# Centring the output projection's weights once, and a residual step without a mean, in an attention and mixture-of-experts block on one Trainium2 core

## The reference, cut to what matters

```python
# x: (8, 512, 256)
x = x + layernorm(attention(layernorm(x)))      # attention ends in: out @ W_o.T
x = x + layernorm(moe_ffn(layernorm(x)))

def layernorm(x, eps=1e-05):
    m = mean(x, -1); v = var(x, -1)
    return (x - m) / sqrt(v + eps)
```

## Time and profile before

| | |
|---|---|
| runs shown | median 965.01 us of 3 (961.19 to 965.33) |
| the profiled execution: its own time | 970.2 us |
| the profiled execution: its span | 968.0 us, mean granted TensorE clock 0.914 |
| busy in the span | PE 811.1 us (84%), DVE 641.1 (66%), ACT 449.8 (46%), POOL 423.0 (44%) |
| DMA | 168.40 MB moved |

### The profile page before, as it was taken

One profiled execution on the slowest core, in us unless ns is written; L12 is line 12 of the kernel. 1 busy time (PEld: TensorE's weight loads), 2 busy tenths in 40 slices (PEclk: granted clock), 3 DMA queues, 4 the chain that ended last, 5 costly groups with the idle time before them and its releaser, 6 DMA issues.

```text
span 968.0 us, 19930 instructions
## 1 busy us (share of the span) xinstructions
PE 811.1 (84%) x6324; PEld 597.3 (62%) x6324; DVE 641.1 (66%) x1850; ACT 449.8 (46%) x731; POOL 423.0 (44%) x408
## 2 busy tenths in 40 slices
PE   3559887887988997897978987989998999888755
PEld 2427464564664764664745555868886888777622
DVE  5686857689688788788687664644643334977616
ACT  2205544645654654654644656545554555444300
POOL 3132213116516427427314335476677655655421
PEclk9758989999998898998997879899999999989878
DMA  4586845335537437436496213554566758888582
GB/s 175 131 206 169 241 92 132 88 88 149 152 99 171 141 98 191 130 85 192 131 334 189 92 49 108 159 182 145 162 213 215 208 163 315 315 289 305 209 348 97
DMA packets 88147, 168.40 MB, mean 174 GB/s; under 512 B 14192, under 2 KB 55664, under 8 KB 87792
## 3 DMA queue, kind: packets, MB, share of 16 engines
q1 hardware_dynamic: 74224, 128.59, 46.0%
q0 software_dynamic: 13824, 38.55, 10.5%
HBM read 90.15 MB, written 76.68 MB: 172 GB/s over the span
## 4 chain that ended last, share of the span: by engine, by line
PE 30%; DVE 9%; DMA 7%; issue 4%; POOL 3%; SPq 3%; ACT 2%; DVEq 0%; POOLq 0%; ACTq 0%
PE ring L1540 9%; PE ring L1561 4%; DMA xg<-sorted_rows 3%; PE ring L1526 2%; DVE nmax L833 2%; POOL expert_rows L736 2%; PE ring L1440 2%; PE ring L1318 2%; PE ring L1320 2%; PE ring L1319 2%; PE ring L1396 2%; DMA q_st<-mrow 2%; DMA expert_rows<-ys,dest 1%; SPq L628 1%; PE ring L1332 1%
## 5 line engine op out<-in xcount | busy, mean ns | idle before, releaser
L736 POOL DMA_INDIRECT expert_rows<-ys,dest x160 | 159.0, 994 | 94.3 <-ACT ys L1199 44.5
L1248 ACT ACTIVATE prob<-ring 128x1024 f32<-128x1024 f32 x128 | 130.1, 1022 | 144.7 <-PE ring L1387 144.3
L833 DVE TENSOR_REDUCE nmax<-ring 128x2 f32<-128x768 f32 (+1 forms) x192 | 158.2, 862 | 26.3 <-PE ring L1369 25.1
L728 POOL DMA_INDIRECT sorted_rows<-xr,idx_all x128 | 126.6, 989 | 96.7 <-DVE xr L995 63.4
L1540 PE MATMUL ring<-we,xh 128*128 x640 | 158.9, 393 | 0.0
L1540 PEld LDWEIGHTS ring<-we,xh 128*128 128x128 f32 x640 | 120.7, 199 | 14.2
L1058 DVE SCALAR_TENSOR_TENSOR sl<-sl,got,ring 128x128 f32<-128x128 f32 x160 | 48.3, 343 | 104.2 <-ACT sl L1300 104.1
L1396 PE MATMUL ring<-prob,v_sb 128*32 128x512 f32 (+3 forms) x1024 | 97.3, 479 | 3.3 <-ACT prob L1248 3.3
L1362 PE MATMUL ring<-k_st,q_st 48*128 48x384 f32 (+3 forms) x512 | 80.4, 374 | 20.9 <-DVE nmax L830 10.3
L706 POOL TENSOR_TENSOR rot<-rot 128x512 f32<-128x512 f32 x14 | 17.9, 1276 | 160.0 <-DVE rot L810 160.0
L1381 PE MATMUL ring<-maskt_b,halves_b 64*128 64x128 bf16 (+2 forms) x640 | 50.7, 238 | 42.2 <-DMA q_st<-mrow 20.7
(11 more groups left out here) (205 smaller groups left out, 1687.7 us busy)
## 6 DMA issues: line engine op xcount, KB each, us to landing
xg<-sorted_rows SPq DMA_DIRECT2D x160, 134.0 KB
parts<-part SPq DMA_DIRECT2D x32, 512.0 KB, 5.8
ykt<-expert_rows SPq DMA_DIRECT2D x14, 1024.0 KB, 10.0
k_st<-parts SPq DMA_DIRECT2D x64, 128.0 KB
q_st<-parts SPq DMA_DIRECT2D x64, 128.0 KB
we<-w_exp SPq DMA_DIRECT2D x1, 6144.0 KB, 21.4
sorted_rows<-zeros SPq DMA_DIRECT2D x2, 2144.0 KB, 9.0
sorted_rows<-zeros SPq DMA_DIRECT2D x32, 134.0 KB
```

The source lines that it names most:

```text
L728: pool.indirect_dma_start(out=xs[group_of(s)], out_offset=bass.IndirectOffsetOnAxis(ap=idx_all[:, s, t, k:k + 1], axis=0), in_=xr[:, s % 2 ...
L736: pool.indirect_dma_start(out=yk, out_offset=bass.IndirectOffsetOnAxis(ap=dest[:, j % 8, b:b + 1], axis=0), in_=ys[:, j % NYS, b, :], in_o ...
L833: dve.tensor_reduce(nmax[:, Q % 2, :, pp, qb], slot[:, :, col:col + (qb + 1) * P], AX.X, ALU.max, negate=True).then_inc(s_max, 1)
L1248: act_e.activation(prob[:, u % 2, 2 * half:2 * half + 2, :], slot[:, :, :], ACT.Exp, scale=SCALE).then_inc(s_exp, 1)
```

## The change

A new function `centre_output_weights` on DVE reduces the `W_o` columns of `stage` (128 partitions, 2 tiles of 256) to their sums, multiplies by 1/256 and subtracts the mean in place. It runs at step "XT" of sequence 0, in the place where `w_lo` was made. ACT's copies to `w_hi` and `w_gate` wait for it and go from step "LNR" to step "QK" of sequence 0. DVE's making of `w_lo` goes from step "XT" to step "V" of sequence 0, which in the plan stands after "LNR" and ahead of "XT" of sequence 1. `residual` becomes four `scalar_tensor_tensor` of 128x256, `x1 = pr * rstd2 + x1`, with both waits ahead of them. The statistics of `pr` stay as they were.

```diff
-N_LN = 5 * NT + 1
+N_LN = 5 * NT
...
             def store_x1(s):
-                sp.wait_ge(s_ln, N_LN * s + 3 * NT + 1)
+                sp.wait_ge(s_ln, N_LN * s + 3 * NT)
...
+            def centre_output_weights():
+                w_o = stage[:, C_O:C_O + KD * D].rearrange("p (k d) -> p k d", k=KD)
+                dve.wait_ge(s_small, 16)
+                dve.tensor_reduce(w_mean[:, 0, :], w_o, AX.X, ALU.add).then_inc(s_centre, 1)
+                dve.wait_ge(s_centre, 1)
+                dve.tensor_scalar(w_mean[:, 1, :], w_mean[:, 0, :], 1.0 / D, None, ALU.mult).then_inc(s_centre, 1)
+                dve.wait_ge(s_centre, 2)
+                dve.tensor_tensor(w_o, w_o, w_mean[:, 1, :].unsqueeze(2).to_broadcast([P, KD, D]),
+                                  ALU.subtract).then_inc(s_centre, 1)
...
             def residual(s):
-                done = N_LN * s + 2 * NT
                 dve.wait_ge(s_lnr, 2 * s + 1)
+                dve.wait_ge(s_x1in, 16 * (s + 1))
                 for t in range(NT):
-                    dve.tensor_scalar(pr[:, t, :], pr[:, t, :], mv2[:, t, 0:1], rstd2[:, t:t + 1],
-                                      ALU.subtract, ALU.mult).then_inc(s_ln, 1)
-                dve.wait_ge(s_x1in, 16 * (s + 1))
-                dve.wait_ge(s_ln, done + NT)
-                dve.tensor_tensor(x1[:, :, :], x1[:, :, :], pr[:, :, :], ALU.add).then_inc(s_ln, 1)
+                    dve.scalar_tensor_tensor(x1[:, t, :], pr[:, t, :], rstd2[:, t:t + 1], x1[:, t, :],
+                                             ALU.mult, ALU.add).then_inc(s_ln, 1)
 
             def residual_statistics(s):
-                done = N_LN * s + 3 * NT + 1
+                done = N_LN * s + 3 * NT
...
                 elif kind == "XT":
                     xt_low(n, ring[RING_SLOT[st]])
+                    if n == 0:
+                        centre_output_weights()
+                elif kind == "V":
                     if n == 0:
                         weights_low(1, slice(C_O, C_GATE), w_hi[:, :], w_lo[:, :])
...
-                elif kind == "LNR" and n == 0:
-                    act_e.wait_ge(s_small, 16)
+                elif kind == "QK" and n == 0 and st[2] == 0:
+                    act_e.wait_ge(s_centre, 3)
                     copy(w_hi[:, :], stage[:, C_O:C_GATE], s_whi)
```

More of the change, by code:

```diff
@@ L328, in block_kernel @@
         r_s = place("r_s", [P, 3, NT])
+        w_mean = place("w_mean", [P, 2, KD])
         cw = place("cw", [P, NT, E])
@@ L400, in block_kernel @@
         s_wlo = sem("weights_low")
+        s_centre = sem("output_weights_centred")
         s_seen_dve = sem("waited_dve")
```

## The result

| | before | changed |
|---|---|---|
| median of 12 runs each | 963.36 us (959.75 to 968.73) | 953.03 us (950.95 to 958.38) |
| ratio, with its 95% interval | | 0.9899 (0.9874 to 0.9923) |
| profiled execution: time, span, clock | 970.2, 968.0, 0.914 | 957.5, 955.3, 0.924 |

The change gains 1.0%. The number came out better than its parts: one term of the sum was too large, the microseconds arrive in other sequences than forecast, and one step of the argument was wrong. Ratios leave out an execution that is over 1.5% above the fastest of its kernel; there is one, in the run with the tiny residual, and it is the one that was profiled.

What follows compares the result with a forecast made beforehand. It took PE and DVE taking turns, with DVE's residual on the path, as the bound. From a median of 965.0 us, -8.4 for seven residuals, +0.4 for the start and -2.6 for the clock gave 954.4, range 948 to 961.

Steps and rivals of the forecast that it cites:

- What bounds the kernel: Steady attention: PE and DVE take turns, the residual lies on the path, with 1.78 us of room on PE's side.
- Sequences 1 to 4 have this same pattern: Periods of sequences 1 to 4: PE waits 1.78 us behind the residual in each, so each saving arrives.
- The residual step: DVE, each residual: 2.62 us before; four multiply-and-adds save 1.26 to 1.06 us, taken as 1.2.
- four new ones move on every 0.34: DVE residual: each new instruction takes a step of 0.34 us, 1.36 us together, from the plain two-tensor operation.
- the far row: Upper bound from a 128x128 multiply-with-pointer with one PSUM operand: 0.39 us per new instruction, four times 1.56.
- The trace does not agree: DVE residual: set aside the skill's rate rule (some 0.5 us less saving per sequence), citing 406 ns against 426.
- How many steps arrive: Eight residuals: the 1.2 us saving arrives in seven, all but sequence 7; 7 x 1.2 = 8.4 us.
- In sequence 7 the saving is nothing: Sequence 7: DVE itself waits 5.28 us for POOL's power, queued behind scatters, so nothing is gained.
- The start: Kernel start: centring and ACT's copy cost 0; moved `w_lo` delays `xt_lo` of sequence 1, +0.4 us, bounds 0 to 2.4.
- The clock: Half-clock stretches behind PE's two waits shrink from 6.6 to 3.4 us in two of five periods: -2.6 us.
- The sum: Whole kernel: -8.4 + 0.4 = -8.0 us, then -2.6 for half-clock stretches; from 965.0 to 954.4 us.
- The slower rival: Every residual meets POOL's two SBUF subtractions on the shared port, 3.3 us instead of 2.62: 970.3 us; chance 0.03.

Runs made afterwards that it cites:

- the tiny residual: The changed kernel with multiply-and-adds on 2 of the 256 channels at each residual; 947.1 us, 0.9817 of the kernel before.
- the filler: The changed kernel with one reduction over 912 elements behind each new residual: 962.32 us, 0.9997 of the kernel before; with two such reductions 975.06 us, 1.0116.
- the start alone: The kernel before with centring and moved weight copies but the old residual; 967.04 us, 1.0042 of the kernel before; run again 966.51 us, 1.0036.
- the two kernels with a later residual: The changed kernel with the residual due at 24.85, not 24.7: 969.09 us, 1.0057 of the kernel before; with statistics and normalised rows later too: 973.63 us, 1.011.

## Why the prediction was right, point by point

- **What bounds the kernel: right.** The residual lay on the path, and the filler shows it from the other side: 1.02 us put back at each residual takes the gain away. The room on PE's side was not the same everywhere, as "Sequences 1 to 4 have this same pattern" has it: in sequence 2 of the profile before, PE ran at half clock from 303.7 to 307.2 and then waited only 0.35 us (at 307.63), not 1.78. The period 2-3 became 1.1 us shorter all the same; the second wait, for line 830, stood there in full (1.97).
- **The residual step: right in kind, one term too large.** "four new ones move on every 0.34" was 0.40 ((1.67 - 0.480) / 3), and the saving 1.02 instead of 1.2, just under my lower bound of 1.06. Seven times that is 7.1 us, not 8.4. I had taken the plain two-tensor operation as nearest and left out that a per-partition scalar has its price; the value from the far row, 0.39, was the better one.
- **"The trace does not agree": wrong.** I set the rule of the Trainium skill (VectorE: DVE Perf Modes, "The perf-mode tier table": `tensor_scalar` at two elements per cycle, `tensor_tensor` at one) aside because the old one took 406 ns and the two-tensor one 426. One size can't tell a rate from a fixed part. The measured growths, 0.40 and 0.80 us for 768 elements, bear the rule out; what the table doesn't give is the 0.13 us for two pointers. By the rule alone the saving would have been some 0.7 us, by my rows 1.2; it was 1.02.
- **How many steps arrive: seven was the wrong picture.** By the table of periods they arrive, with what the clock adds, in sequences 0 to 4 and 6; in sequence 5, for which I had counted a whole one, nothing can be told. Sequence 0 saved 0.9 of its own (4.53 to 3.63). "In sequence 7 the saving is nothing", with DVE's wait longer by the saving, failed: the wait is 5.07 instead of 5.28. POOL's power runs 10.58 us behind the residual's start (625.93) where before it was 11.15 (638.31), because a scatter issue ahead of it in POOL's queue is no longer drawn out by the old addition. With the filler, which is a reduction and no addition, it is 10.58 too. I had priced the port between DVE and POOL in one direction only.
- **The start: harmless, but not by the step I gave.** +0.4 us was forecast, since `w_lo` would end near 39.15 and hold `xt_lo`. DVE came to `w_lo` at 35.87, 0.9 us sooner than I had placed it, for a reason that is not traced, and `xt_lo` ends at 39.45, no later than before. The first residual stands at 161.84 against 161.47, but the kernel before alone gave 161.47 in one profile and 160.13 in another. With the old residual the same start costs 3.5 us, most of it at the addition of sequence 2.
- **The clock: the right kind and size, not the right places.** PE's granted clock is 0.50, 1.2 GHz, behind the two waits before. I had taken shorter stretches for two of five residuals. In the means of three profiles the time at half clock is 3.4 us less in periods 1-2 and 6-7 and 4.6 less in 3-4, but 1.9 more in 4-5 and 5.0 more in 5-6. Single stretches prove little: behind the residual of sequence 5 it is gone in the second profile of the kernel before as well. The whole is a mean of 148 to 153 us for the kernel before in its sets of runs, 135 for the changed one, 151 with one filler, 173 with two, 123 with the tiny residual. Between runs of one kernel a microsecond more at half clock goes with -0.08 to 0.28 us more of span, by which set of 12 or more runs is taken; 13 to 18 us less are worth up to some 5 by that, where I had 2.6. That is an estimate and no proof.
- **The sum.** Mine was 8.4 - 0.4 + 2.6 = 10.6. Seven times the measured 1.02 is 7.1, which leaves 3.2 of the 10.3 us for the clock and sequence 7; that is a subtraction, and how the gain splits stays open. That the total came out within half a microsecond is partly luck: the instruction was overestimated, sequence 5 brought nothing, and sequence 7, the start and the clock brought more than I had.
- **The slower rival: the mechanism is real.** I put the point at who starts first, the residual or POOL's pair. It is met in sequence 0 of every kernel but the tiny one, in sequence 2 of the start alone, and in sequences 0 to 4 of the two kernels with a later residual. The Trainium skill, SBUF — State Buffer, "SBUF: two separate sides", calls this an exclusive lock between the two engines, which whoever starts first keeps for its whole instruction. The runs agree that one engine stands while the other works. Who started first can't be read from the profile's starts alone: the addition at 305.54 started 0.44 us ahead of the pair and still waited for it, and with the later residual a multiply-and-add of 0.48 us started at 234.28, 0.61 ahead of the pair, and ended at 237.70. In both cases POOL was already in the scatter issue that the pair follows without a gap (305.00 and 233.91). Whether that issue holds the port was not tested by itself.

## What to carry to other kernels

To tell what an instruction of another form will cost, take rows of two sizes: one size can't tell a rate from a fixed part, and here it hid both a doubled rate and 0.13 us for two pointers. Before a step on VectorE is shortened, lengthened or moved, look how far GpSimd's next two-tensor operation on SBUF stands from it, and what GpSimd runs ahead of that: here a residual made 1.2 us later turned a gain of 1.0% into a loss of 0.6%. A gain that is summed over periods should be looked for period by period, in more than one profile. And when a part that should cost nothing costs something, look for the one instruction whose maximum is far from its median; the place may have nothing to do with the edit.

## What was not expected of the hardware

- DVE can lose to a whole run of POOL's operations and not to one: 4.03 us for an addition of 1.23 with 2.49 us of the pair beside it, 3.4 us at most for one multiply-and-add of 0.48 in the kernels with a later residual. In sequence 0 they take turns instead: the third and fourth of the four take 1.5 us each (their maximum is 1507 ns), one for each operation of the pair.
- A small shift decides it in the old code: in all profiles the addition kept its 1.23 where the pair started 0.74 us or more behind it, and the pair was drawn out to 2.84; where it started 0.44 or 0.46 behind, the addition lost 2.8. This is no general threshold: the multiply-and-add at 234.28 lost with 0.61.
- POOL loses too: the issue of a scatter took 1.67 us instead of 0.96 beside an addition of 128x1024 on DVE.
- An instruction of 4 elements is held up as well (0.19 to 1.26 us), while the statistics of 128x256 that ran partly beside the pair (230.94) kept their 1.39 for four.
